# Transformer block with a sparse mixture of experts: the FFN of three rows on the two chosen experts alone

## What is computed

```python
logits = jnp.tanh(xt @ Wg1.T) @ Wg2.T
_, top_idx = jax.lax.top_k(logits, K)                      # K = 2 of E = 8
top_scores = softmax(take_along_axis(logits, top_idx))
scores = zeros_like(logits).at[rows, top_idx].set(top_scores)
up = einsum('td,ehd->teh', xt, Wup) + bup                   # 256 -> 8 x 128
h = silu(up)
down = einsum('teh,eoh->teo', h, Wdown) + bdown             # 8 x 128 -> 256
out = einsum('te,teo->to', scores, down)
x = x + gb * out                                            # gb: one vector per row
```

## Time and profile before

| | |
|---|---|
| time, median of 3 runs | 487.5 us (483.69 to 488.05) |
| span of the profiled execution | 486.4 us |
| PE busy | 445.4 us (92%) |
| DVE, ACT, POOL busy | 275.7, 152.5, 88.7 us |
| time that the transfers took | 11.6% of the 16 DMA engines |
| all matmuls of `up` (L1447) and `down` (L1464) | 63.0 and 63.3 us busy |

### The profile page before, as it was taken

The page is one execution under the profiler, slowest core; times in us unless marked ns, Lnnn a source line. Parts: engine busy times, 40 slices in busy tenths (PEclk is TensorE's granted clock), DMA queues, the critical chain, the costliest instruction groups (busy, mean ns, idle before and its releaser), DMA issues.

```text
span 486.4 us, 8167 instructions
## 1 busy us (share of the span) xinstructions
PE 445.4 (92%) x3258; PEld 278.5 (57%) x3258; DVE 275.7 (57%) x559; ACT 152.5 (31%) x244; POOL 88.7 (18%) x101
## 2 busy tenths in 40 slices
PE   7798789988899999999999999899989788899887
PEld 4475334656466565546766555466666556674265
DVE  4835678978974778567225687671325544213431
ACT  1547675423323435232114353331031221012300
POOL 1202003320224024201021060120211420003000
PEclk9797999999899999999999999999999897699889
DMA  7960000000001000000024000000240000003000
GB/s 262 366 209 0 1 0 1 3 3 1 2 3 45 2 1 1 3 0 3 0 79 141 3 1 2 1 4 0 77 142 3 1 3 1 13 22 98 1 11 32
DMA packets 15992, 18.76 MB, mean 39 GB/s; under 512 B 1676, under 2 KB 14252, under 8 KB 15940
## 3 DMA queue, kind: packets, MB, share of 16 engines
q1 hardware_dynamic: 15940, 18.04, 11.6%
HBM read 15.94 MB, written 2.10 MB: 37 GB/s over the span
## 4 chain that ended last, share of the span: by engine, by line
PE 67%; DVE 20%; issue 5%; ACT 4%; DMA 1%; POOL 1%; SPq 0%; DVEq 0%; POOLq 0%; ACTq 0%
PE ps L1299 16%; PE ps L1464 13%; PE ps L1447 9%; DVE conv L990 8%; PE ps L1404 5%; PE ps L1378 3%; PE ps L1365 3%; PE ps L1326 2%; PE ps L1225 2%; PE ps L1461 2%; PE ps L1346 2%; PE ps L1454 1%; PE ps L1415 1%; PE ps L1259 1%; ACT conv L855 1%
## 5 line engine op out<-in xcount | busy, mean ns | idle before, releaser
L1299 PE MATMUL ps<-hT,win 128*128 128x512 f32 x256 | 128.1, 627 | 5.5 <-DVE conv L990 4.5
L990 DVE SCALAR_TENSOR_TENSOR conv<-ps,small,conv 128x511 f32<-128x511 f32 x144 | 107.0, 747 | 37.9 <-ACT conv L855 34.6
L1299 PEld LDWEIGHTS ps<-hT,win 128*128 128x128 f32 x256 | 46.8, 197 | 50.8 <-issue 41.6
L1447 PE MATMUL ps<-hT,wup 128*128 128x512 f32 x128 | 63.0, 619 | 1.4 <-ACT sT L924 1.4
L1464 PE MATMUL ps<-wdg,hs 128*128 128x256 f32 x256 | 63.3, 403 | 0.0
L855 ACT ACTIVATE conv<-ps,small 128x512 f32<-128x512 f32 x48 | 37.2, 775 | 76.2 <-PE ps L1299 76.2
L1464 PEld LDWEIGHTS ps<-wdg,hs 128*128 128x128 f32 x256 | 50.0, 200 | 12.5 <-issue 5.3
L1196 DVE TENSOR_TENSOR x<-ps,x 128x256 f32<-128x256 f32 x16 | 6.8, 424 | 72.2 <-PE ps L1464 72.2
L935 ACT ACTIVATE hs<-ps,bup 128x512 f32<-128x512 f32 x32 | 22.0, 686 | 66.8 <-PE ps L1447 66.8
L1447 PEld LDWEIGHTS ps<-hT,wup 128*128 128x128 f32 x128 | 23.0, 194 | 24.3 <-issue 20.6
L784 ACT ACTIVATE conv<-conv 128x512 f32<-128x512 f32 x48 | 29.7, 622 | 15.8 <-DVE conv L990 15.7
(11 more groups left out here) (124 smaller groups left out, 504.3 us busy)
## 6 DMA issues: line engine op xcount, KB each, us to landing
wdg<-w_down_T SPq DMA_DIRECT2D x4, 1024.0 KB, 5.6
conv<-x SPq DMA_DIRECT2D x4, 512.0 KB, 7.5
wog<-w_out_T SPq DMA_DIRECT2D x4, 512.0 KB, 4.1
x<-x SPq DMA_DIRECT2D x4, 512.0 KB, 8.5
out<-x SPq DMA_DIRECT2D x16, 128.0 KB, 1.7
win<-w_in_T SPq DMA_DIRECT2D x2, 512.0 KB, 7.8
hs<-w_mod SPq DMA_DIRECT2D x1, 1024.0 KB, 10.2
win<-w_in_T SPq DMA_DIRECT2D x1, 1024.0 KB, 12.4
```

The costliest lines, as they stand in the source:

```text
L990: dve.scalar_tensor_tensor(out=dst, in0=bank(("proj", b, m))[:, 0:SEQ - s], scalar=cw[:, m, KSIZE - 1 - s:KSIZE - s], in1=dst, op0=ALU.mul ...
L1299: ins = pe.matmul(bank(step), win[:, k, m * P:(m + 1) * P], hT[:, k, b * SEQ:(b + 1) * SEQ], start=(k == 0), stop=(k == KD - 1))
L1447: ins = pe.matmul(bank(step), wup[:, k, e * P:(e + 1) * P], hT[:, k, b * SEQ:(b + 1) * SEQ], start=(k == 0), stop=(k == KD - 1))
```

## The change

Row 3 keeps the dense FFN. For rows 0 to 2 each token gives two pairs (token, chosen expert), 3072 pairs in all.

- The normalised and modulated tokens are made a second time in token layout (`hb`): `hdiag` and `hmod` spread the modulation vectors over the partitions, and POOL computes `xn * hm0 + hm1` for each of 12 tiles (`scaled_row`).
- `rank` counts by five small bf16 matmuls how many tokens before each one chose the same expert, and DVE turns this into a slot: expert times 1536 plus the count. `scat` writes the token rows of 1 KB to their slots in a DRAM buffer `pair_rows` (12288 rows of 1 KB, 12.6 MB), with 8 indirect transfers of 128 rows per row of the batch, issued by POOL. The whole buffer has been filled with zeros by one transfer from SP near the start.
- `plan` works out how many tiles of 128 pairs each expert has, and writes a table of 31 tiles: first row in `pair_rows`, and expert. 31 tiles are the most there can be; always 31 are computed.
- SP reads the table entry by entry (`value_load`) and issues for each tile one load of 128 rows (128 KB) and one of the expert's up and down weights (`w_pair`, 256 KB), into rings of 8 tiles. It starts when all 24 scatters of the three rows have landed.
- The pair work goes by quads of 4 tiles: `gt` transposes (8 per quad), `gu` is the up product (two matmuls of 128 columns per tile) with silu on ACT, `gd` the down product (one matmul of 256 columns per tile), a copy on DVE and a store to a DRAM buffer `pair_out`, two tiles at a time. These 40 steps stand from tile 2 of row 3's scan on, between the rest of the scan and row 3's gate steps, and after them.
- `comb`: for each of 12 tiles of 128 tokens POOL issues two indirect gathers of 128 rows of `pair_out`, and DVE combines them in 4 operations with the scores and the gate vector and adds them to the residual. The bias of the down product is added by `bias` (two matmuls with 8 rows, twice per row).
- Row 3's dense `up`, `bc` and `down` stand behind all pair work, since its buffer `hs` holds the ring of pair weights. `wup` and `wdg` are now loaded late, once, into the space of the input weights. `up`, `bc` and `down` of rows 0 to 2 and the reloads of `wdg` are gone.

```diff
@@ -44,9 +44,20 @@
...
 
+N_SPARSE = 3
+PICKS = 2
+REGION = N_SPARSE * SEQ
+N_PAIR_TILE = (PICKS * REGION + N_EXP * (P - 1)) // P
+N_SLOT = N_EXP * REGION
+QUAD = 4
+N_QUAD = -(-N_PAIR_TILE // QUAD)
+RING = 8
...
+
+
+def take(steps, count=1):
+    return [steps.pop(0) for _ in range(min(int(count), len(steps)))]
+
...
-        if word == "p":
-            out += take(nxt)
-        elif word.isdigit():
@@ -315,15 +388,68 @@
...
+        yg = lent0[:, 0:RING * DM].rearrange("p (r k d) -> p r k d", k=PICKS, d=DM)
+        base = RING * DM
+        hg = lent0[:, base:base + 4 * SEQ].rearrange("p (r k t) -> p r k t", r=2, k=KD)
+        hq = lent0[:, base + 4 * SEQ:base + 6 * SEQ].rearrange("p (r t) -> p r t", r=2)
+        ysb = lent0[:, base + 6 * SEQ:base + 8 * SEQ].rearrange("p (r t) -> p r t", r=2)
+        plan_a = cmp_[:, :, :, :].rearrange("p i a b -> p (i a b)")
+        plan_b = eq[:, :, :, :].rearrange("p i a b -> p (i a b)")
@@ -651,44 +796,78 @@
...
+            sp.dma_start(rt[:, :], route_d).then_inc(ld["route"], 16)
+            sp.wait_ge(zrow_made, 1)
+            n_fill = N_SLOT // P
+            sp.dma_start(xs_d.rearrange("(t p) d -> p t d", p=P),
+                         zrow[:, None, :].to_broadcast([P, n_fill, DM])).then_inc(filled, 16)
...
+            def load_rows(q):
+                if q >= 2:
+                    wait_bank(sp, ("gt", q - 2, KD - 1))
+                for t in quad_tiles(q):
+                    row = sp.value_load(tab[0:1, 0, t:t + 1])
+                    sp.dma_start(xg[:, t % RING, :], xs_d[bass.ds(row, P), :]).then_inc(ld_xg[t % RING], 16)
+
+            def load_weights(q, h):
+                if q >= 2:
+                    wait_bank(sp, ("gd", q - 2, h))
+                for t in quad_tiles(q, h):
+                    e = sp.value_load(tab[0:1, 1, t:t + 1])
+                    sp.dma_start(wt[:, t % RING, :], pairw_d[bass.ds(e, 1)].rearrange("o p w -> (o p) w")
+                                 ).then_inc(ld_wt[t % RING], 16)
+
+            def store_pairs(q, h):
+                tiles = quad_tiles(q, h)
+                n = 2 * q + h
+                sp.wait_ge(ysb_ready, n + 1)
+                sp.dma_start(ys_d.rearrange("(t p) d -> p t d", p=P)[:, tiles[0]:tiles[-1] + 1, :],
+                             ysb[:, n % 2, 0:len(tiles) * DM].rearrange("p (t d) -> p t d", d=DM)
...
+            sp.dma_start(wdg, wdn_d.rearrange("e p n -> p e n")).then_inc(ld_wd, 16)
+            sp.wait_ge(plan_ready, 2)
+            sp.wait_ge(scattered, 16 * N_SPARSE * PICKS * TPB)
+            for q in range(2):
+                load_rows(q)
+                for h in range(2):
+                    load_weights(q, h)
+            for q in range(N_QUAD):
+                if q + 2 < N_QUAD:
+                    load_rows(q + 2)
+                for h in range(2):
+                    store_pairs(q, h)
+                    if q + 2 < N_QUAD:
+                        load_weights(q + 2, h)
@@ -704,6 +883,24 @@
...
+            def scaled_row(m):
+                b, i = divmod(m, TPB)
+                pool.wait_ge(xn_ready, N_TILE + m + 1)
+                pool.wait_ge(hm_ready, b + 1)
+                if i == 0 and b >= 2:
+                    pool.wait_ge(scattered, 16 * PICKS * TPB * (b - 1))
+                r = hb[:, b % 2, i, :]
+                link(pool.tensor_tensor(r, xn[:, m % 4, :], hm[:, 0, :], ALU.mult))
+                pool.tensor_tensor(r, r, hm[:, 1, :], ALU.add).then_inc(hb_ready, 1)
@@ -760,16 +961,44 @@
...
+                elif kind == "scat":
+                    b = step[1]
+                    pool.wait_ge(filled, 16)
+                    pool.wait_ge(slot_ready, b + 1)
+                    pool.wait_ge(hb_ready, TPB * (b + 1))
+                    for i in range(TPB):
+                        for k in range(PICKS):
+                            pool.indirect_dma_start(
+                                xs_d, bass.IndirectOffsetOnAxis(routed(sloti, b, k, i), 0), hb[:, b % 2, i, :], None,
+                                bounds_check=N_SLOT - 1, oob_is_err=False).then_inc(scattered, 16)
...
+                    b, i = step[1:]
+                    n = tile_no(b, i)
+                    if n == 0:
+                        pool.wait_ge(yslot_ready, 1)
+                        for r in range(2):
+                            pool.wait_ge(stored_pair[r], 16 * N_QUAD)
+                    if n >= 4:
+                        pool.wait_ge(comb_done, n - 3)
+                    for k in range(PICKS):
+                        pool.indirect_dma_start(
+                            yg[:, n % 4, k, :], None, ys_d, bass.IndirectOffsetOnAxis(routed(ysloti, b, k, i), 0),
+                            bounds_check=N_PAIR_TILE * P - 1, oob_is_err=False).then_inc(gathered[n % 4], 16)
@@ -867,11 +1096,36 @@
...
+                elif kind == "gt":
+                    q = step[1]
+                    for k in range(KD):
+                        wait_bank(act, step + (k,))
+                        if q >= 2:
+                            wait_bank(act, ("gu", q - 2, 1))
+                        w = len(quad_tiles(q)) * P
+                        act.activation(hg[:, q % 2, k, 0:w], bank(step + (k,))[:, 0:w], ACT.Copy).then_inc(hg_ready, 1)
+                elif kind == "gu":
+                    q, h = step[1:]
+                    wait_bank(act, step)
+                    act.wait_ge(bupt_ready, 1)
+                    if q >= 2:
+                        wait_bank(act, ("gd", q - 2, h))
+                    for t in quad_tiles(q, h):
+                        cols, own = (slice(t % n * P, (t % n + 1) * P) for n in (QUAD, 2))
+                        act.activation(hq[:, q % 2, cols], bank(step)[:, own], ACT.Silu,
+                                       bias=bupt[:, t:t + 1]).then_inc(hq_ready, 1)
@@ -1176,22 +1457,105 @@
...
+                elif kind == "rank":
+                    b = step[1]
+                    wait_bank(dve, ("rk", b))
+                    dve.wait_ge(ld["route"], 16)
+                    dve.tensor_tensor(slf[:, :, :], bank(("rk", b))[:, 0:TPB * N_EXP].rearrange("p (i e) -> p i e", e=N_EXP),
+                                      ebase[:, None, :].to_broadcast([P, TPB, N_EXP]), ALU.add).then_inc(slotf_ready, 1)
+                    dve.wait_ge(slotf_ready, b + 1)
+                    link(picked(b, slf, slot))
+                    dve.tensor_copy(of_row(sloti, b), of_row(slot, b)).then_inc(slot_ready, 1)
+                    link(dve.tensor_reduce(mrow[:, :], mk[:, :, :].rearrange("p i e -> p e i"), AX.X, ALU.add))
...
+                    b, i = step[1:]
+                    n = tile_no(b, i)
+                    y0, y1 = yg[:, n % 4, 0, :], yg[:, n % 4, 1, :]
+                    r = x1_tile(b, i)
+                    dve.wait_ge(gathered[n % 4], 16 * PICKS * (n // 4 + 1))
+                    dve.wait_ge(s01_ready, N_SPARSE)
+                    dve.wait_ge(bias_added, 2 * N_SPARSE)
+                    link(dve.tensor_scalar(y0, y0, routed(s01, b, 0, i), None, ALU.mult))
+                    link(dve.scalar_tensor_tensor(out=y0, in0=y1, scalar=routed(s01, b, 1, i), in1=y0,
+                                                  op0=ALU.mult, op1=ALU.add))
+                    link(dve.tensor_tensor(y0, y0, gates[:, 1 + b, :], ALU.mult))
@@ -1312,6 +1676,73 @@
...
+                elif kind == "bias":
+                    b, h = step[1:]
+                    wait_bank_free(pe, step)
+                    pe.wait_ge(bdg_ready, b + 1)
+                    pe.wait_ge(sT_ready, b + 1)
+                    for j in range(2):
+                        ins = pe.matmul(bank(step)[:, j * DM:(j + 1) * DM], sT[:, tile_cols(2 * h + j)], bdg[:, b % 2, :],
+                                        start=True, stop=True)
+                    ins.then_inc(full[bank_of[step]], 1)
+                elif kind == "gt":
+                    q = step[1]
+                    for k in range(KD):
+                        job = step + (k,)
+                        wait_bank_free(pe, job)
+                        for t in quad_tiles(q):
+                            if k == 0:
+                                pe.wait_ge(ld_xg[t % RING], 16 * (t // RING + 1))
+                            ins = pe.transpose(bank(job)[:, tile_cols(t % QUAD)], xg[:, t % RING, k * P:(k + 1) * P], ident)
+                        ins.then_inc(full[bank_of[job]], 1)
+                elif kind == "gu":
+                    q, h = step[1:]
+                    wait_bank_free(pe, step)
+                    pe.wait_ge(hg_ready, KD * (q + 1))
+                    for t in quad_tiles(q, h):
+                        pe.wait_ge(ld_wt[t % RING], 16 * (t // RING + 1))
+                        for k in range(KD):
+                            ins = pe.matmul(bank(step)[:, tile_cols(t % 2)], wt[:, t % RING, k * P:(k + 1) * P],
+                                            hg[:, q % 2, k, tile_cols(t % QUAD)], start=(k == 0), stop=(k == KD - 1))
```

(10 more changed lines are left out.)

470 lines of the change are left out of this document (374 added, 96 removed).

## The result

The changed kernel took 472.1 us (median, 469.4 to 477.3) beside 487.8 us of the kernel before: a ratio of 0.969, 95% interval 0.962 to 0.976. The span of the profiled execution is 471.8 us. 467 had been predicted, with a range of 446 to 505. The ratios, and the medians in the table of experiments, leave out executions over 1.5% above the fastest of the same kernel, among them the profiled ones of g0, g2, g3 and k1.

What follows compares the result with a forecast made beforehand. PE bounds the scans; SP was to pace the pair phase, 343 to 419 us. Products end at 422.5, the dense end at 460, the last store at 462.7; 3 for the clock gives 465.7, and 1.1 to the median 467, range 446 to 505.

Steps and rivals of the forecast that it cites:

- Row 3, tiles 0 and 1: Start of row 3's scan: tile 0 takes 19.6 us and tile 1 15, so tile 2 starts at 334.6 us.
- g, the indirect transfers: Issue time of each scatter or gather on POOL: 1.09 us, so 8.7 for eight scatters and 26.2 for 24 gathers.
- rival 2: Indirect transfers on POOL are dearer: 505 us at 1.9 us each, 522 at 2.35; chance 0.11.
- c, a load on SP: Pair phase: each of 62 loads costs SP 1.09 us for reading, arithmetic and issue, 67.6 us in all.
- rival 1: SP's reading, arithmetic and issue per pair load are dearer: 499 us at 1.6 us per load; chance 0.14.
- SP is the later one; PE stalls and it costs nothing: Pair phase: PE stalls at the quads' transposes at no cost, as SP's 76 us, to 419, end later.
- The dense end: Row 3's `up`, `bc`, `down` after the pair work: 33.5 us plus 2 and 2 for slow starts, to 460.
- Hidden behind the dense end by 5.7 us: Gathers and combining run from 424.8 to 454.3 us, beside row 3's dense products, ending 5.7 us before them.
- 3: The scans do not shorten: rows 1 and 2 stay at about 86 us, total 479 us; chance 0.10.
- 4: The zero fill is slow and delays row 0's `out`: 487 us at 150 GB/s, 530 at 100; chance 0.05.
- rival 5: SP's reading and issue are cheaper, 0.6 us per load: the end comes at about 445 us; chance 0.06.
- Rival 6: Indirect transfers pass one at a time, at least 1.7 us each: total 481 us; chance 0.04.

Runs made afterwards that it cites:

- g0: The changed kernel run again, unaltered, on a second chip: 471.0 us, 0.974 of the kernel before.
- g2: Changed kernel with two of the four DVE operations of each combination left out: 470.7 us, 0.970 of the kernel before.
- g3: Changed kernel with 14 matmuls on zeros added on PE in row 3's first three tiles: 475.6 us, 0.979 of the kernel before.
- k1: Changed kernel with SP reading several table entries per instruction, 24 table loads instead of 62: 472.4 us, 0.962 of the kernel before.
- k0: The changed kernel run unaltered a third time, on a third chip: 476.1 us, 0.972 of the kernel before.
- f1: Changed kernel with the 62 pair loads going to fixed rows and experts, without table reads on SP: 467.6 us, 0.965 of the kernel before.
- f2: Changed kernel with pair weights loaded for the first 8 tiles only, 23 loads fewer: 465.0 us, 0.961 of the kernel before.
- k2: Changed kernel with batched table reads and SP's loads issued ahead of the stores that wait for copies: 467.0 us, 0.954 of the kernel before.
- f4: Changed kernel without row 2's 8 scatters, its pairs computed on zeros: 469.9 us, 0.965 of the kernel before.

## Why the prediction was right, and where it was not

The likeliest case came out, 5 us above its value. The step by step comparison is less flattering: several errors cancel, and that the sum came so close is in part luck.

- *The scans.* Row 0 was costed at +1 us and took 59.3 for 60.7 us. Rows 1 and 2: predicted 79.6 and 80.7, measured 79.7 and 82.1. Row 3's start: 300, measured 299.1. That DVE would keep its 58.7 us in row 1 was right (60.5). This part carries the whole gain.
- *Row 3, tiles 0 and 1.* 19.6 and 15 us predicted, 19.9 and 18.6 measured. The step that failed is "plus 4 because logits, ranks, scores and `spread` now follow at once": it was 7.3. The chain was priced with PE's links at full clock, and they ran at the low level: `out` took 3.75 us for 1.9. The low clock was allowed for only with 3 us for the pair phase. SP was released at 346.8 for 343.
- *g, the indirect transfers.* Predicted 1.09 each. The busy time is right (1.01 and 1.03 us), but 0.30 us pass before the next: 1.31 apart. I had not added a gap on POOL although SP's issues had one. Row 2's eight scatters took 10.1 us for 8.7. At the end it decides: the gathers took 33.3 us for 26.2, so the point named in rival 2, 1.33, from which they overtake the dense products, was reached in effect.
- *c, a load on SP.* Predicted 1.09 us, measured about 0.80 for rows (four issues in 2.73 us) and 0.96 for weights: 54.6 us for 67.6. The read was the mis-sized part, 0.27 us for 0.67; the bound from the flag contained a semaphore and a matmul's start, as rival 1's counterargument says. What took its place is waiting: 8.7 us for copies up to the last load instead of 3 (13.3 in k0), and single issues of up to 1.48 us for 0.33. SP's phase was 71 us for 76. "SP busy without a break" is therefore wrong. It delays PE, as f1 and f2 show, but in good part through its order, as k2 shows: the loads stand behind waits for copies of tiles already done.
- *"SP is the later one; PE stalls and it costs nothing".* PE's sum of 34 + 30 + 5 = 69 us was about right (67 to 70), though a tile of pairs costs 1.35 us (`gu` 1.06 and `gd` 1.13 for two, `gt` 1.04 for four) and not 1.1. Wrong was that it costs nothing: with PE at 69 and SP at 71 us a stall of the one is never quite made up by the other, and the stretch took 80. The last products ended 8.5 us after SP's last load, where I had 3.5.
- *The dense end.* Predicted 37.5 us and 3 for the clock, measured 34.3 (426.4 to 460.7): no first `down` was slow, because there was no pause ahead of it. The 5.34 us of the earlier trace rows belong to a pause that the new order doesn't have.
- *The end.* "If the kernel ends in a combination rather than a `down`, a step above is wrong": it did, 7 us behind the last `down`. "Hidden behind the dense end by 5.7 us" failed by four terms: the last store landed 3.8 us behind the last pair matmul instead of 2.3, the gathers took 7 us more, the dense end was shorter, and DVE's 20 us of combinations do not lie beside the dense products but start 13.4 us late and then set the pace together with the gathers.
- *The fill.* Costed at nothing, and right: issued at 12.1 us, landed 44.3 us later, with 380 to 386 GB/s in the slices from 24 to 47 us, over by 57 us for the 60 predicted. But SP could issue nothing behind it for 40 us: its next small load stands at its issue from 12.57 us for 39.96, and the output weights were issued at 54.99. Row 0's `out` did not need them sooner. No experiment was made on it.
- *The rivals.* 1, 3 and 4 are excluded by the rows above. Of rival 5 the condition came half true, 0.88 us per load for 1.09, but its time of 445 did not. The upper end of the range was taken from rival 2 at g = 1.9 as 505; its own prices (24 x 0.81 + 24 x 0.57 on 467) give 500. Rival 6, transfers one at a time: a gather takes 2.9 us from issue to landing (median in k0) and the next starts 1.31 us after it, so they overlap. The Trainium skill (DMA: Bandwidth & Descriptors, "Anatomy of one DMA — SWDGE (gpsimd) path") is borne out in its fixed cost of about 2 us for one transfer, and it does not add up over transfers in a row.

## What to carry to other kernels

A queue that issues loads and stores should never let a load stand behind a store's wait for data: this order was worth about 5 us here (k2 beside k1), at least as much as making the issuing itself cheaper, and it doesn't show in the queue's busy time, only in the waits of the engine that it feeds. When two chains end within a few us of each other, price both and their gaps from one operation to the next; taking half of one away gives only the distance to the other. Before moving issues to an engine with spare time, look at what stands behind them there. Before taking two profiles for a comparison, see that the stages ahead of the one compared ran at the same clock: f4's gain was hidden by 2.4 us in an earlier tile.

## What the runs showed of the hardware

**Indirect transfers on POOL** of 128 rows of 1 KB cost 0.97 to 1.25 us each with 0.30 between, with DVE busy 60 of 80 us beside them. The Trainium skill (SBUF — State Buffer, "Who interferes with whom") has VectorE, in a mode that takes both ports, holding up the descriptors of such transfers; in these 48 it can be no more than the 0.28 us between the shortest and the longest. What the rows do agree with is its rule for two computing engines, that a VectorE instruction with two inputs in SBUF contends with a GpSimd instruction that reads SBUF. The write of the tile table in the changed kernel, beside POOL's product from 344.67 to 345.76 us:

```profile
344.67 1.09 POOL L950 TENSOR_TENSOR xv<-xtok,fv 128x512 f32<-128x512 f32 x1
...
344.69 1.14 DVE L1508 SCALAR_TENSOR_TENSOR tab<-rt,tsh 128x31 int32<-128x31 f32 x1
```

and in k1, where an indirect transfer stands there:

```profile
344.80 1.00 POOL L979 DMA_INDIRECT pair_rows<-hs,sloti  x1 [0.30 <-issue]
...
345.88 0.19 DVE L1511 SCALAR_TENSOR_TENSOR tab<-rt,tsh 128x31 int32<-128x31 f32 x1
```

**Reading a register from SBUF on SP** took 0.27 us in the median (0.26 to 1.11), several entries at once 0.47. The Trainium skill (DMA: Bandwidth & Descriptors, "Latency and other measured facts") gives a floor of about 0.6 us; the rows are below it.

**The clock early in the program** moves whole executions by 5 us. The same 32 matmuls in the changed kernel and in k0:

```profile
24.51 3.68 PE L1623 MATMUL ps<-win,hT 128*128 128x64 f32 x32
```

```profile
25.15 6.93 PE L1623 MATMUL ps<-win,hT 128*128 128x64 f32 x32
```

The granted clock from 24 to 36 us was 1.00 in one and 0.58 in the other, and row 0's scan began at 78.4 and 83.5 us. Both kinds occur with one and the same kernel. That is as much as the differences sought here, and why stretch and tail are compared above and not only the totals.
